# Delta rule in a decoder kernel: output products moved between the successor's steps and reads, chain at 9.3, wait for copied outputs at the additions

## The reference

```python
K = K / jnp.maximum(jnp.linalg.norm(K, axis=-1, keepdims=True), EPS)
def step(W, inp):
    q_t, k_t, v_t, b_t = inp
    pred = jnp.einsum('bhij,bhj->bhi', W, k_t)
    err = v_t - pred
    W_new = W + b_t[..., None, None] * jnp.einsum('bhi,bhj->bhij', err, k_t)
    o_t = jnp.einsum('bhij,bhj->bhi', W_new, q_t)
    return (W_new, o_t)
...
out = jnp.moveaxis(O, 0, 1).reshape(B, T, H * D)
return out @ Wout
```

## Time and profile before

| what | us |
|---|---|
| median of 3 runs | 1770.65 |
| lowest and highest | 1768.19, 1773.63 |
| the profiled execution | 1778.7 |
| its span, first to last instruction | 1776.9 |
| the chain stretch in it (first to last output product) | 1191.8 to 1648.0 |
| mean granted TensorE clock | 0.937 |

### The profile page before, as it was taken

One profiled execution on the slowest core, in us unless ns is written; L12 is line 12 of the kernel. 1 busy time (PEld: TensorE's weight loads), 2 busy tenths in 40 slices (PEclk: granted clock), 3 DMA queues, 4 the chain that ended last, 5 costly groups with the idle time before them and its releaser, 6 DMA issues.

```text
span 1776.9 us, 41801 instructions
## 1 busy us (share of the span) xinstructions
PE 1543.4 (87%) x18044; PEld 814.6 (46%) x18044; DVE 1215.7 (68%) x2341; ACT 914.8 (51%) x1269; POOL 681.2 (38%) x716
## 2 busy tenths in 40 slices
PE   7887878789999999999988988888889899898985
PEld 3222222333334333433423544677777778675552
DVE  7788875777774776667545667765876775475766
ACT  1676654566774777577574333355445444333220
POOL 1111100355564655466473104467855557000000
PEclk9899997899999999999998998799999998879998
DMA  4000002222322222223120100000000001100000
GB/s 149 1 1 1 1 1 81 84 70 81 99 81 58 81 70 78 60 85 100 39 69 14 62 1 13 13 15 4 15 15 16 15 4 35 49 2 1 6 7 12
DMA packets 32408, 70.65 MB, mean 40 GB/s; under 512 B 5328, under 2 KB 7056, under 8 KB 31968
## 3 DMA queue, kind: packets, MB, share of 16 engines
q1 hardware_dynamic: 32224, 67.98, 13.1%
HBM read 47.45 MB, written 20.51 MB: 38 GB/s over the span
## 4 chain that ended last, share of the span: by engine, by line
PE 59%; DVE 28%; ACT 6%; issue 5%; POOL 1%; DMA 0%; DVEq 0%; ACTq 0%; POOLq 0%; SPq 0%
PE ps L159 56%; DVE a_MX L407 5%; DVE b_mx L844 3%; PE ps L227 1%; DVE st L171 1%; PE ps L1533 1%; DVE b_VL L791 1%; POOL b_EL L916 1%; ACT d_L L168 1%; DVE sq L206 1%; DVE st L197 1%; DVE d_XE L1656 1%; DVE X L203 1%; DVE d_AT L1935 1%; DVE a_QS L171 1%
## 5 line engine op out<-in xcount | busy, mean ns | idle before, releaser
L916 POOL TENSOR_TENSOR b_EL<-b_X,b_EH 128x1024 f16<-128x1024 f32 x160 | 341.1, 2132 | 312.3 <-ACT b_EH L168 312.3
L844 DVE TENSOR_REDUCE b_mx<-ps 128x2 f32<-128x666 f32 x256 | 217.0, 848 | 102.3 <-PE ps L159 102.1
L898 ACT ACTIVATE b_X<-ps 128x1024 f32<-128x1024 f32 x160 | 163.8, 1024 | 133.9 <-PE ps L159 132.9
L1719 POOL TENSOR_TENSOR d_tmp<-d_G,d_XI 128x31 f32<-128x31 f32 (+15 forms) x248 | 128.1, 517 | 194.2 <-DVE d_G L1648 175.4
L168 ACT ACTIVATE b_EH<-b_X 128x1024 f16<-128x1024 f32 x160 | 169.1, 1057 | 27.9 <-PE ps L159 16.7
L444 ACT ACTIVATE a_E<-ps 128x1024 f32<-128x1024 f32 x128 | 131.2, 1025 | 97.1 <-PE ps L159 96.5
L159 PE MATMUL ps<-b_M,b_S 128*128 128x512 f16 (+1 forms) x768 | 177.1, 384 | 2.0 <-ACT b_X L898 1.9
L407 DVE TENSOR_REDUCE a_MX<-ps 128x2 f16<-128x1024 f32 x128 | 155.4, 1226 | 30.4 <-PE ps L159 29.1
L1722 POOL TENSOR_TENSOR d_XI<-d_XI,d_tmp 128x31 f32<-128x31 f32 (+15 forms) x248 | 141.5, 571 | 19.5
L159 PE MATMUL ps<-b_Hk,b_Hq 64*128 64x333 f16 x512 | 83.3, 322 | 38.5 <-DVE b_mx L844 35.1
L426 POOL TENSOR_TENSOR a_QS<-a_QS,a_MR 128x512 f16<-128x512 f16 x16 | 18.5, 1154 | 234.1 <-ACT a_MR L168 234.1
(11 more groups left out here) (324 smaller groups left out, 3354.0 us busy)
## 6 DMA issues: line engine op xcount, KB each, us to landing
b_S<-s_xk SPq DMA_DIRECT2D x48, 336.0 KB, 6.3
b_M<-s_xq SPq DMA_DIRECT2D x48, 256.0 KB, 5.0
s_xk<-b_Hk SPq DMA_DIRECT2D x16, 336.0 KB, 2.2
s_xk<-b_Lk SPq DMA_DIRECT2D x16, 336.0 KB, 2.5
s_xq<-b_Hq SPq DMA_DIRECT2D x16, 256.0 KB, 2.0
s_xq<-b_Lq SPq DMA_DIRECT2D x16, 256.0 KB, 2.0
d_XI<-eye SPq DMA_DIRECT2D x8, 512.0 KB, 4.2
f_w<-f_w SPq DMA_DIRECT2D x1, 2048.0 KB, 8.2
```

Source lines behind the costliest of these rows:

```text
L844: v.e.tensor_reduce(out, PS[:, bk:bk + 2, 0:333], AX, ALU.max).then_inc(sem("b_mx"), 1)
L898: a.e.activation(b_X[k % 2], PS[:, bk:bk + 2, :], ACT.Exp, scale=0.125).then_inc(sem("b_ex"), 1)
L916: last = p.e.tensor_tensor(b_EL[k % 6], b_X[k % 2], b_EH[k % 6], ALU.subtract)
L1719: e.tensor_tensor(tm, a, x, ALU.mult).then_inc(*p.step())
```

## The change

Three edits, all in the order. On TensorE the empty chain step before the output products is dropped, so that they are step 8. The chain's number in every weave is 9.3 for 9. On VectorE the wait for the copied outputs (`d_o`) stands no longer ahead of the first chunk but ahead of the additions into `d_OT` after chunks 3 and 7. With this the output products of unit u are due at 8/9.3 = 0.860, between the steps (14/17 = 0.824) and the reads (16/17 = 0.941) of unit u+1; before, they were due at 1, between reads and outputs.

```diff
@@ d_chain_tensor
                 if cc % 4 == 3:
                     last.then_inc(sem("d_sq2"), 1)
                 yield
-            yield
             t.wait_ge("d_ot", 2 * u + 2)
             t.wait_ge("d_add", b)
             for k in range(4):
@@ d_chain_vector
             v.wait_ge("d_b", 2 * u + 2)
-            v.wait_ge("d_o", 2 * u + 2)
             for cc in range(1, 8):
...
                 if cc % 4 == 3:
                     h, w = cc // 4, 64 * (1 - cc // 4)
                     x = d_OT[j][:, :, 256 * h + w:256 * h + 256]
+                    v.wait_ge("d_o", 2 * u + 2)
                     v.wait_ge("d_sq2", 2 * u + h + 1)
@@ d_order
-                streams = [(chain(lane, u), 9)]
+                streams = [(chain(lane, u), 9.3)]
```

## The result

The changed kernel is slower. Its median over 20 runs is 1776.47 us, against 1768.55 us over 20 runs of the kernel before: a ratio of 1.0042, with a 95% interval of 1.0023 to 1.0061. The forecast was 1770.5 us and no measurable change. The time is outside its range, and slower had a chance of 0.12. Run once more beside the last of the experiments, the same kernel gave 1.0080 (1.0053 to 1.0106).

A forecast was written before the change was run, and what follows sets the result against it. TensorE, busy for 87% of the span, was taken as the bound, with VectorE's full queue behind many of its waits. The terms summed to -0.25 us on 1770.65, rounded to 1770.5 us, range 1763.5 to 1776.

The forecast's parts named there:

- b: Chain density 9.3 for 9, chunks 6 and 7 earlier: +1.1 us in weaves 0, 1, 11, 12, +0.5 in weave 3.
- c: Output products before reads: +0.2 us in weave 6, +0.7 in 12, +0.15 in 7, -1.65 in 13, +0.75 in 15.
- the clock: Low clock behind weave 11's 1.99 us wait, priced at 4.0 us and left out of the sum.
- Rival D: Slower: chunk 6 ahead of last solve waits longer in weaves 3, 5, 9; 2.9 us, 6.9 with low clock; chance 0.12.
- a: Wait for copied outputs moved to the chain's additions on VectorE: pays in weave 11, -1.5 us.
- d: TensorE's "issue" stops in weaves 1, 3 and 7: bounds -1.3 and +1.7 us, taken as -0.5.
- Rival B: Faster by the clock: weave 11's low clock goes with the removed wait, -4.0 us, to 1766.5; chance 0.16.

The follow-up runs named there:

- e2_dense: The kernel before with only the chain's density changed, 9.3 for 9, on both engines; ratio 1.0032, +5.6 us.
- i1_chunk6: The kernel before with one swap on TensorE, chunk 6 ahead of the last solve; ratio 1.0060, +8.5 us by the medians.
- h1: The kernel before with the d_o wait moved, density 9.3 on VectorE alone, output products early in weave 13 alone; 1763.76 us, ratio 0.9989.
- h2: The kernel after with density 9 again on TensorE alone, output products early in every weave; 1771.76 us, ratio 1.0029.
- f1_hold: The kernel after with unused matmuls of ones put ahead of the output products in weaves 2, 4, 6, 8 and 10; ratio 1.0026.
- e3_early: The kernel before with only the output products one step earlier, between steps and reads, at density 9; ratio 1.0133.
- e6_late: The kernel after with the output products put back between reads and outputs; moved d_o wait and density 9.3 stay; ratio 1.0027.

## Why the prediction was wrong

**The forecast fell in two of its steps, b and c, and by what it left out, the clock.** Rival D came true in its sign, but only in part by its mechanism: in the kernel after chunk 6 waits 2.75 us in weaves 1 to 10 for 1.04 before, where rival D had 2.9 more, and its low clock behind these waits did not come.

*a. Right.* Weave 11 in the kernel after: the chunk waits for nothing, and the corner step waits 0.85 us for the d_OT copy (0.5 had been reckoned), so 1.1 us of the 1.5 are in the trace.

```profile
1480.42 1.08 ACT L168 ACTIVATE d_OT<-ps 128x512 f32<-128x512 f32 x2
...
1481.07 1.20 PE L159 MATMUL ps<-d_XE,d_L 32*32 32x32 f32 x64 [0.85 <-ACT d_OT L168]
```

*b. Wrong.* The step said: +0.28 us in weaves 0, 1, 11 and 12, 0.5 in weave 3, and nothing in weaves 5 and 9, where the later waits would close up. It was mis-sized: 1.6 us in the sum, and 5.6 measured in e2_dense. The waits themselves were foreseen. This is TensorE in weave 5 of the kernel after the earlier trace rows:

```profile
1325.98 0.45 PE L159 MATMUL ps<-d_S,d_AT 64*64 64x64 f32 x8 [1.37 <-DVE d_S L1997]
...
1326.49 1.04 PE L159 MATMUL ps<-d_KV,d_XE 64*64 64x128 f32 x16
...
1328.32 0.93 PE L159 MATMUL ps<-d_KV,d_UW 64*64 64x64 f32 x48 [0.56 <-ACT d_UW L168]
...
1330.12 2.05 PE L159 MATMUL ps<-d_wo,d_OT 128*128 128x128 f32 x16
```

1.25 and 0.5 us had been reckoned, 1.37 and 0.56 came, and the waits for chunk 7 and the products are gone. (The other wait above 1 us came in weave 7 and not in weave 9.) What failed is the addition of waits as if all were alike. The old waits of 0.73 and 0.78 us stood behind the transitions, and VectorE and ScalarE worked under them. The new ones stand ahead of the last solve and of the transitions, on which d_UW, d_L, d_G and d_AT hang, so everything after them is late; that this makes up the rest of the 5.6 us is argued and not measured by itself. Weave 7 had such a wait too (1.38 us) and was not in the sum. And in the even weaves, for which the step had nothing, the copy d_UW of the last solve has ScalarE's d_L copy behind it. That queue was not followed: VectorE's five waits for d_L rose from 9.7 to 12.0 us in the kernel after, as they did in i1_chunk6. The lost cover of 0.28 us was priced in weaves 0, 1, 11 and 12 alone. The trace of the kernel after has the reads of chunk 7 alone between the last solve and the transitions in the even weaves too (weave 4 above); in 15 weaves it would be 4.2 us, an estimate from the two rows of the prediction.

*c. Right at the edges, wrong in the middle.* The hole of weave 13, 4.42 us, was to become 2.7. It became 2.17 + 0.57 = 2.74 us:

```profile
1553.94 0.44 PE L159 MATMUL ps<-d_QT,d_S 64*64 64x64 f32 x7 [0.57 <-DVE d_S L1997]
...
1558.24 2.05 PE L159 MATMUL ps<-d_wo,d_OT 128*128 128x128 f32 x16 [2.17 <-DVE d_OT L2003]
```

The f_wo products wait 0.69 us for the Gelu, for 0.75 reckoned:

```profile
1652.17 3.84 PE L159 MATMUL ps<-f_wo,f_HT 128*128 128x128 f32 x32 [0.69 <-ACT f_HT L2447]
```

In the even weaves the waits for d_AT did change their name. The step gave them the same sum after it, near 8 us; at the same five places the additions show 10.4. Where the step had 0 in weaves 2, 4, 8 and 10 and 1.05 us in weaves 6, 7 and 12, the pair h1 and h2 shows 8.0 us, over all weaves but 13. The 2.05 us by which the reads are later were set against VectorE's backlog at d_QT alone. They come out at the d_OT copies and the next chain, two queues further on.

*d. Right in sign.* The waits of "issue" fell by 5.1 us, more than the bound of 1.3. Little of it shows in the time, as the waits of other names in the same stretch rose.

*The clock.* The prediction left it out of the sum, as such waits bring the low clock on only at times. Over all runs the kernels with the products early in every weave and no ones ran at a mean clock of 0.9419 (70 runs, standard error 0.0006), all others but f1_hold at 0.9458 (140 runs, 0.0003). By the slope above, 0.0039 are 3.5 us, an estimate: the slope is a correlation between runs of one kernel. f1_hold lies at 0.9453, which suggests the waits ahead of the products as the cause; its standard error is 0.0013, so it is not shown. The test that the prediction set, a clock within 0.02 from 1160 to 1650 us, was passed (0.93 in both profiles) and too coarse to see this. Rival D had put the low clock behind chunk 6's waits. There it is not: no stretch of low clock in weaves 1 to 10 of any profile stands behind one, the longest of them 1.42 us, and the profile of i1_chunk6 kept 0.99.

Rival B's mechanism shows too. Behind the wait of 1.99 us in weave 11 the clock was low for 10.2 us in the kernel before, and as long in the two other profiles that have this wait, e3_early and i1_chunk6. In the kernel after it is low there for 3.4 us, behind the products' wait of 1.92 us, and in no other profile for longer than that. So the 4.0 us that the prediction priced and left out came back in large part in the profile, and b and c lost more than the total shows.

The Trainium skill (TensorE: Matmul & The Clock Gate, A second HAM failure mode) tells of a kernel in which frequent short idle times between groups of matmuls made the clock go back and forth. The traces agree: each dip in weaves 1 to 10 of any profile stands behind a wait.

## What to carry to other kernels

A wait costs by its place: weigh it by what hangs on the step behind it, on every engine, and not by its length. A step that fills the latency of a copy should not be moved ahead of the work that the copy follows unless another takes its place: a moved step of 0.49 us cost 8.5 us here, over 15 rounds of a loop. Test the parts of an order change alone and in pairs, and by runs enough to see 0.2%: here the two parts that seem to pay (a, and c in weave 13) were hidden by the two that don't.

## What the hardware showed

Over the 20 profiles, 62 stretches of low clock start in weaves 1 to 10, and each one within a wait of TensorE of at least 1.2 us or at most 2.3 us behind its end, though such waits and the 3.1 us behind them make up less than a fifth of the time. How often a wait has one behind it rises with its length:

```
wait, us      1.2-1.6   1.6-2.0   2.0-2.3   2.3 and more
waits              74        40        36        41
with low clock      6        10        21        25
```

It stays a matter of chance: e6_late had waits of 3.0 and 2.8 us in weaves 2 and 6 and no low clock in the ten weaves. The price is small: 17 us more at 1.2 GHz went with 4.9 us more of busy time in the kernel after, 0.3 us for each us.

Stops of "issue" change with the order as well. Weave 5 of i1_chunk6 has one of 1.37 us amid the reads, where the kernel before shows none and waited 0.78 us for data a little later.
